# A linear attention block with an FFN on one core: another opening, the first two FFNs in tile 3, and another order in the last three tiles

## The reference, cut to what matters

```python
def attention(x, W_attn, b_attn, W_proj, b_proj):        # x: 8 x 1024 x 512
    q, k, v = split(x @ W_attn + b_attn, 3)               # 16 heads of 32
    q, k = elu(q) + 1, elu(k) + 1
    # over the tokens t of a sequence:
    #   kv += k_t (outer) v_t ; ksum += k_t
    #   y_t = (q_t . kv) / (q_t . ksum + 1e-6)
    return y @ W_proj + b_proj

def ffn(x, weight, bias):
    x16 = clip(x, -448, 448).astype(float8_e4m3fn).astype(float16)
    w16 = clip(weight, -448, 448).astype(float8_e4m3fn).astype(float16)
    return (x16 @ w16.T).astype(float32) + bias

x = x + attention(layernorm(x), ...)
x = x + ffn(layernorm(x), ...)
```

## Time and profile before

| what | value |
|---|---|
| median of 3 executions | 950.37 us (949.42 to 951.35) |
| the profiled execution's own time | 948.85 us |
| its span, first to last instruction | 947.1 us |
| TensorE busy | 918.2 us, 97% |
| DVE, ACT, POOL busy | 731.8, 745.6, 641.3 us (77, 79, 68%) |
| DMA moved | 99.12 MB, mean 105 GB/s |

### The profile page before, as it was taken

The page is one execution under the profiler, slowest core; times in us unless marked ns, Lnnn a source line. Parts: engine busy times, 40 slices in busy tenths (PEclk is TensorE's granted clock), DMA queues, the critical chain, the costliest instruction groups (busy, mean ns, idle before and its releaser), DMA issues.

```text
span 947.1 us, 44776 instructions
## 1 busy us (share of the span) xinstructions
PE 918.2 (97%) x19470; PEld 490.5 (52%) x19532; DVE 731.8 (77%) x1404; ACT 745.6 (79%) x1358; POOL 641.3 (68%) x713
## 2 busy tenths in 40 slices
PE   5998999999999999999999999999999999999896
PEld 2455555555555555555555555555555555555454
DVE  6999879787777777778687687777778687676687
ACT  5788787877869688787877868788787878868874
POOL 5659877766767677676776667677676676764433
PEclk9999999999999999999999999999999999999999
DMA  8926564565464554565555465555555455462421
GB/s 268 143 41 109 109 119 103 97 119 97 95 122 100 98 116 104 96 114 105 95 114 107 91 116 106 89 118 108 92 114 112 89 114 110 90 103 59 76 69 59
DMA packets 252036, 99.12 MB, mean 105 GB/s; under 512 B 232384, under 2 KB 232640, under 8 KB 251840
## 3 DMA queue, kind: packets, MB, share of 16 engines
q1 hardware_dynamic: 251840, 96.25, 52.3%
HBM read 22.81 MB, written 16.78 MB: 42 GB/s over the span
## 4 chain that ended last, share of the span: by engine, by line
PE 90%; POOL 3%; issue 2%; ACT 2%; DVE 2%; SPq 1%; DMA 1%; ACTq 0%; POOLq 0%
PE R L235 77%; PE S L235 13%; POOL st L1029 1%; POOL xn L1031 1%; DMA x2t<-x2b 0%; ACT raw L477 0%; POOL xs L1076 0%; PE R L239 0%; DVE raw L739 0%; POOL raw L1062 0%; DMA xs<-in_L_attn_x 0%; ACT ktok L477 0%; SPq L1227 0%; DVE v L728 0%; ACT o L477 0%
## 5 line engine op out<-in xcount | busy, mean ns | idle before, releaser
L235 PE MATMUL R<-xt,wh 128*128 128x512 f16 x1024 | 306.2, 381 | 2.4 <-ACT wh L477 2.4
L716 DVE SCALAR_TENSOR_TENSOR qk<-qk,rel 128x512 f32<-128x512 f32 x128 | 112.8, 884 | 118.1 <-ACT rel L489 118.1
L477 ACT ACTIVATE raw<-qk 64x512 f32<-64x512 f32 x256 | 160.8, 628 | 48.9 <-PE S L235 45.7
L235 PE MATMUL R<-xt,wl 128*128 128x512 f16 x512 | 194.0, 380 | 0.0
L1083 POOL TENSOR_TENSOR yhl<-y,yhl 128x512 f16<-128x512 f32 x60 | 70.0, 1167 | 146.1 <-ACT yhl L477 146.1
L235 PE MATMUL R<-wh,xt 128*128 128x512 f16 x512 | 158.0, 379 | 0.0
L235 PEld LDWEIGHTS R<-xt,wh 128*128 128x128 f16 x1024 | 96.7, 98 | 116.0 <-DVE xt L882 2.6
L739 DVE TENSOR_TENSOR raw<-S,causal 64x1024 f32<-64x1024 f32 x128 | 155.9, 1218 | 0.9
L1029 POOL TENSOR_TENSOR st<-st,half 128x1 f32<-128x1 f32 x127 | 92.7, 730 | 90.6 <-DVE st L705 89.8
L235 PE MATMUL R<-wph,yt 128*128 128x512 f16 (+1 forms) x520 | 132.4, 377 | 3.9 <-ACT yt L477 1.9
L486 ACT ACTIVATE qk<-R,bqk,wm 128x512 f32<-128x512 f32 x128 | 98.9, 773 | 35.6 <-PE R L235 35.0
(11 more groups left out here) (108 smaller groups left out, 1364.8 us busy)
## 6 DMA issues: line engine op xcount, KB each, us to landing
xs<-in_L_attn_x SPq DMA_DIRECT2D x64, 256.0 KB, 3.1
out<-xs SPq DMA_DIRECT2D x63, 256.0 KB, 2.4
raw<-in_L_attn_W_attn SPq DMA_DIRECT2D x3, 1024.0 KB, 9.5
xs<-in_L_attn_W_proj SPq DMA_DIRECT2D x4, 256.0 KB
raw<-in_L_ffn_weight SPq DMA_DIRECT2D x1, 1024.0 KB, 17.0
raw<-raw SPq DMA_TRANSPOSE x63, 3.7
x2t<-x2b SPq DMA_TRANSPOSE x62, 2.5
xt<-xnhl SPq DMA_TRANSPOSE x60, 3.5
```

The costliest lines, as they stand in the source:

```text
L235: return e.matmul(out, a, b, start=start, stop=stop, skip_group_check=True)
L477: return e.activation(out, in_, ACT.Copy, **more)
L716: e.scalar_tensor_tensor(qk[j % 2][:, i, :], qk[j % 2][:, i, :], 1.0, rel[:, (u - 1) % 2, :], ALU.min, ALU.add).then_inc(s_phi, 1)
```

## The change

- **Opening.** The attention weight comes in four pieces (256, 256, 512 and 512 columns) with a size and a scale each instead of three, and its high and low parts are made in eight parts (four of 128 columns, four of 256). TensorE does warming transposes of the identity (16, 3 and 4) around the first four tiles' transposes, and `most(1)` inside the first product. ACT and DVE have a new order.
- **Tiles 0 to 3.** On ACT in tile 0 one feature product goes ahead of the projection's high part, and the third feature product and `values(0)` ahead of `queries(1)`. On DVE `proj_weight` goes from tile 0 to tile 1, `ffn_high` to tile 1, `ffn_round` to tile 2; the four sums go to POOL in tile 2. `t_wf` goes to SyncE's tile 3, behind `t_k(5)`; `ffn(0)` is done in tile 3 with `ffn(1)` on TensorE, ACT and DVE. The stores of tiles 0 to 2 are issued in tile 4 and the load of tile 14 in tile 5.
- **POOL's add_bp** is done once a tile in tiles 1 to 7 and twice in tiles 8 to 15, instead of twice in 0 to 7.
- **Last three tiles.** DVE does yt's low part and y ahead of v's result, and the FFN's residual sum one tile later; `ln2(61)` goes to tile 63. POOL does `spread(63)` ahead of `proj(61)`, and stores follow one tile later.

```diff
+PIECES = ((0, 256), (256, 512), (512, 1024), (1024, 1536))
+
+PARTS = ((0, 128), (128, 256), (256, 384), (384, 512), (512, 768), (768, 1024), (1024, 1280), (1280, 1536))
...
@@ TensorE
-                        pe.wait_ge(s_wl, i // 2 + 1)
+                        pe.wait_ge(s_wl, part_of(i) + 1)
...
                     if i == j == 0 and m == 8:
+                        most(1)
                         pe.wait_ge(s_wl, 1)
...
-            for m in range(4):
-                t1(m)
+            warm(16)
+            t1(0)
+            t1(1)
+            warm(3)
+            t1(2)
             most(0)
+            t1(3)
+            warm(4)
             for i in range(12):
                 proj_qkv(0, i)
-                if i in (0, 2, 11):
-                    most((0, 2, 11).index(i) + 1)
+                if i in (1, 4, 11):
+                    most((1, 4, 11).index(i) + 2)
...
-                elif 2 <= n < NT - 1:
+                elif n == 3:
+
+                    ffn(0)
+                    ffn(1)
+                elif 4 <= n < NT - 1:
                     ffn(n - 2)
@@ ACT
             t1(0)
             t1(1)
+            attn_size(0)
             t1(2)
-            attn_size(0)
             t1(3)
             attn_weight(0)
             attn_weight(1)
             attn_size(1)
-            phi(0, 0)
+            attn_size(2)
             attn_weight(2)
             attn_weight(3)
+            phi(0, 0)
+            attn_weight(4)
             phi(0, 1)
+            attn_weight(5)
...
-                    ahead(chunks(n)[0])
+                    if n == 0:
+                        ahead(chunks(n)[0][:1])
+                        proj_weight()
+                        ahead(chunks(n)[0][1:])
+                        k_tokens(n + 1)
+                        ahead(chunks(n)[1])
+                        values(n)
+                        queries(n + 1)
+                        ln1_parts(n + 8)
+                    else:
+                        ahead(chunks(n)[0])
@@ DVE, opening
             t1_parts(0)
             t1_parts(1)
+            scale(0)
             t1_parts(2)
-            scale(0)
             t1_parts(3)
             attn_weight(0)
             attn_weight(1)
-            v_peak()
             scale(1)
+            attn_weight(2)
+            attn_weight(3)
+            scale(2)
+            phi(0, 0)
             ln1(4)
-            attn_weight(2)
-            phi(0, 0)
-            attn_weight(3)
+            attn_weight(4)
             ln1(5)
             phi(0, 1)
-            scale(2)
+            v_peak()
+            attn_weight(5)
             phi(0, 2)
+            scale(3)
+            phi(0, 3)
             ln1(6)
-            attn_weight(4)
-            phi(0, 3)
+            attn_weight(6)
+            phi(0, 4)
+            attn_weight(7)
             ln1(7)
-            attn_weight(5)
-            phi(0, 4)
-            v_scale()
             phi(0, 5)
             phi(0, 6)
+            v_scale()
             phi(0, 7)
@@ DVE, main loop
                 if n < NT:
+                    if n == 1:
+                        ahead(chunks(0)[1])
                     if not tail(n):
                         scores(n)
+                    if n == 1:
+                        proj_weight()
                     if n + 8 < NT:
                         ln1(n + 8)
-                    if n == 0:
-                        proj_weight()
                     if n == 1:
-                        ffn_sum(0, 2)
+                        ffn_high()
+                    if n == 2:
+                        ffn_round()
+                    if tail(n - 1):
+
+                        t_y(n - 1)
+                        if n == NT - 1:
+                            ln2(n - 2)
+                        values(n)
                     ahead(chunks(n)[0])
-                    if tail(n - 1):
-                        t_y(n - 1)
                     if n:
                         ahead(chunks(n)[1])
-                    values(n)
-                    if n == 0:
-                        ffn_high()
-                        ffn_round()
-                        ahead(chunks(n)[1])
+                    if tail(n - 1):
+                        if n < NT - 1:
+                            ffn(n - 3)
+                    else:
+                        values(n)
                 if 1 <= n < NT:
                     proj(n - 1)
                 if n == NT - 1:
+                    ffn(n - 3)
                     t_y(n)
-                if 1 <= n < NT:
+                if 1 <= n < NT and n != NT - 2:
                     ln2(n - 1)
@@ POOL
+            def ffn_sum(f):
+                pool.wait_ge(s_wfd, 3)
+                e.tensor_tensor(w_b[:, f, :], w_hi[:, f, :], w_lo[:, f, :], ALU.add).then_inc(s_wfs, 1)
...
+                    if n == 2:
+                        ffn_sum(0)
+                        ffn_sum(1)
                     if n:
                         values(n)
...
                 if 1 <= n < NT:
                     add_bf(n - 1)
+                if n == 2:
+                    ffn_sum(2)
+                    ffn_sum(3)
@@ SyncE
             def t_wf(f):
-                sp.wait_ge(s_wfd, 4 + f)
+                sp.wait_ge(s_wfs, f + 1)
...
-                if n == 1:
-                    t_wf(0)
-                    t_wf(1)
                 if n + 2 < NT:
                     t_k(n + 2)
...
                 if n == 1:
                     t_y(n)
-                    t_wf(2)
-                    t_wf(3)
-                if n + 10 < NT:
+                if n == 3:
+                    for f in range(4):
+                        t_wf(f)
+                if n == 5:
+                    load_x(n + 9)
+                if n != 4 and n + 10 < NT:
                     load_x(n + 10)
```

More of the change, by code:

```diff
@@ L141, in build @@
         Y = S[:, :, 4 * HALF:4 * HALF + 4 * W]
-        UN = [wm[:, 7 * i + 4:7 * i + 5] for i in range(4)]
-        UP = [wm[:, 7 * i + 5:7 * i + 6] for i in range(4)]
-        UN_V, UN_P = wm[:, 33:34], wm[:, 34:35]
+        UN = [wm[:, 7 * i + 4:7 * i + 5] for i in range(5)]
+        UP = [wm[:, 7 * i + 5:7 * i + 6] for i in range(5)]
+        UN_V, UN_P = wm[:, 41:42], wm[:, 42:43]
         raw_p = xs[:, NX - 4:NX, :]
@@ L162, in build @@
         s_out = [sem(f"xo{i}") for i in range(NX)]
-        s_wa = [sem(f"wa{i}") for i in range(3)]
+        s_wa = [sem(f"wa{i}") for i in range(4)]
         s_wf, s_wp, s_bqk, s_bva, s_bias = sem("wf"), sem("wp"), sem("bqk"), sem("bva"), sem("bias")
@@ L187, in build, with weights @@
         s_rs1, s_xn, s_rs2, s_x2, s_xb, s_x1b = sem("rs1"), sem("xn"), sem("rs2"), sem("x2"), sem("xb"), sem("x1b")
-        s_yl, s_blank, s_one, s_khl, s_near = sem("yl"), sem("blank"), sem("one"), sem("khl"), sem("near")
+        s_wfs, s_yl, s_blank, s_one, s_khl, s_near = sem("wfs"), sem("yl"), sem("blank"), sem("one"), sem("khl"), sem("near")
         bank = {}
+        def weights(first, end):
+            third, at = divmod(first, D)
+            return raw[:, third, :, at:at + end - first]
         def four(t):
@@ L500, in proj_size @@
                 act.wait_ge(s_wp, 64)
-                e.activation(wpl[:, :, :].bitcast(BF16), raw_p, ACT.Abs, accum_out=wm[:, 21:22]).then_inc(s_size, 1)
+                e.activation(wpl[:, :, :].bitcast(BF16), raw_p, ACT.Abs, accum_out=wm[:, 28:29]).then_inc(s_size, 1)
             def attn_weight(i):
-                cols = slice(i * 256, (i + 1) * 256)
-                of = slice(i % 2 * 256, i % 2 * 256 + 256)
-                act.wait_ge(s_up, i // 2 + 1)
-                copy(wh[:, :, cols], raw[:, i // 2, :, of], scale=UP[i // 2]).then_inc(s_wh, 1)
+                piece = piece_of(PARTS[i][0])
+                act.wait_ge(s_up, piece + 1)
+                copy(wh[:, :, slice(*PARTS[i])], weights(*PARTS[i]), scale=UP[piece]).then_inc(s_wh, 1)
             def proj_weight():
-                act.wait_ge(s_up, 4)
-                copy(wph[:, :, :], raw_p, scale=UP[3]).then_inc(s_wph, 1)
+                act.wait_ge(s_up, 5)
+                copy(wph[:, :, :], raw_p, scale=UP[4]).then_inc(s_wph, 1)
             def ffn_half():
-                act.wait_ge(s_wl, 4)
+                act.wait_ge(s_wl, part_of(7) + 1)
                 act.wait_ge(s_wfc, 4)
@@ L687, in _ @@
                     spread(n + 1)
-                if 2 <= n <= NT and not (n < NT - 1 and tail(n)):
+                if n == 3:
+                    ffn(0)
+                    ffn(1)
+                elif 4 <= n <= NT and not (n < NT - 1 and tail(n)):
                     ffn(n - 2)
@@ L933, in ffn_round @@
                                 saturate=False).then_inc(s_wfd, 1)
-            def ffn_sum(first, end):
-                dve.wait_ge(s_wfd, 3)
-                for f in range(first, end):
-                    e.tensor_tensor(w_b[:, f, :], w_hi[:, f, :], w_lo[:, f, :], ALU.add).then_inc(s_wfd, 1)
             e.memset(pair[:, :], 0.0).then_inc(s_pair, 1)
@@ L1020, in _ @@
```

(28 more changed lines are left out.)

98 lines of the change are left out of this document (46 added, 52 removed).

## The result

The changed kernel takes 958.05 us (median of 4 runs, 957.0 to 959.05) where the kernel before took 950.86 us in runs of the same chip (4 runs, 949.42 to 951.57). The ratio is 1.0073, 95% interval 1.0057 to 1.009: **slower by 7 us**, where I forecast 3.6. The profiled execution has a span of 956.2 us and its own time is 957.9.

The account below looks back on a forecast made before the run. The prediction took TensorE to bound the kernel, so only its idle or slow time counts. Front +3.1, clock +2.0 and last tiles -1.5 gave +3.6 us on the median of 950.37: 954.0 us, range 947.5 to 958.5.

Parts of the forecast that it names:

- the step that decides: Tile 3: TensorE, at ffn(0) at 99.5, waits 8.0 us for the FFN weight's transposes, there at 107.5.
- Opening: Up to the k transposes: DVE's list ends at 42.4 instead of 44.60, a gain of 2.3 us, bounds 0.8 and 4.
- whether the clock came up or not: Opening: the 2.3 us gain was claimed to hold with TensorE's clock fast or slow.
- Tile 2's two waits: TensorE's waits at tile 2's masked scores (1.22 us) and first FFN (1.25 us) were both to go.
- proj_weight (L916, 2.34 us) goes to tile 1: Tiles 0 to 2: this move adds 2.34 us to DVE's stretch in tile 1, with y at 73.3.
- The clock: Behind tile 3's long wait: TensorE's matmuls run slow, costing 2.0 us, bounds 0 and 2.07.
- The tail: Last tiles: yt's low part first on DVE removes a TensorE wait, -1.5 us, bounds -0.5 and -2.3.
- the 1.18 us gap stays nearly whole: Last tiles: TensorE's wait at 929.04 for ACT's yt stays almost unchanged, as ACT's queue ends just ahead of it.
- In time: Rival: t_k(5) is through before 94, the FFN weight lands before TensorE's 99.5, total 944.1 us; chance 0.16.
- The clock stays up: Rival: tile 3's long wait is there but TensorE's clock doesn't fall, total 952.0 us; chance 0.16.
- the opening gives nothing: Rival: DVE stays where it was in the opening, smaller pieces come later, total 955.5 to 957 us; chance 0.12.

Follow-up runs that it names:

- e10: The changed kernel once more, with no edit, on another chip: 957.63 us, ratio 1.0081.
- e7: e5 with DVE's v_scale behind the last feature product instead of ahead of it: 950.64 us, ratio 1.0012.
- e9: e5 without the 23 warming transposes: 952.05 us, ratio 1.0021.
- e1: The changed kernel with the four FFN weight transposes ahead of t1(11) and t_k(5) in SyncE's tile 3: 948.51 us, ratio 0.998.
- e5: e1 with POOL's spread(1) moved ahead of k_split(2) and the low part of tile 8 in tile 0: 947.22 us, ratio 0.9974.
- e2: The changed kernel with 64 warming transposes on TensorE ahead of ffn(0) in tile 3: 956.82 us, ratio 1.0073.
- e4: The kernel before with only the new order of the last tiles: 948.14 us, ratio 0.9986.
- e11: e5 with the last tiles as before the change: 948.14 us, ratio 0.9977.
- e6: e5 with 12 more warming transposes on TensorE ahead of the k transposes in tile 0: 950.67 us, ratio 1.0009.
- e8: The kernel before with only the warming transposes (16, 3 and 4) and the summing matmul behind the fourth tile's transposes: 951.09 us, ratio 1.0012.

## Why the prediction was right, and where its sizes were off

The direction was right, and so was the step that decides; the size was half: +3.6 us forecast, +7.2 and +6.9 measured by the medians. That 958.05 lies in the range at all is in part luck: my upper end of 958.5 was there for a rival that didn't happen, and the forecast by itself went to 957. I go by e10's profile, whose span is 7.3 us above that of before, 6.7 of it in front of update(4) and 0.6 behind it.

- **Opening, right in size: -2.2** (k transposes 42.51 in e10, 42.97 in the first; forecast 42.4). DVE's list is the last to end, as argued, from its first scale at 11.2 (10.7 forecast) to 42.4, with 2.8 us idle (2.4 forecast), but by less than a microsecond: e7 takes 3.8 us out of its way and wins 0.17, or about 0.8 with the executions' difference taken off. And "whether the clock came up or not" was wrong. e9 puts the price of the clock at 3.1 us at this point. I had taken DVE's list as a chain that TensorE doesn't touch; in fact each feature product waits for TensorE's projection through ACT, so slow projections delay the same list. It was the wait between the engines that I had wrong. Without the fast level the new opening would have been 1 us worse than the old.
- **Tile 2's two waits, right:** 1.22 and 1.25 us are gone, in every kernel with the new order.
- **"proj_weight (L916, 2.34 us) goes to tile 1": the step that failed.** I priced this move, and ffn_high's, as time of DVE alone. Beside them POOL's low part and spread(1) take 2.67 and 2.77 us instead of 1.15 and 0.62, and TensorE's values(1) waits 1.46 us for the latter (e10, e1); e5 takes the wait away by reordering POOL alone. What I said of ACT's moved values and queries held: ACT's high part of y ends at 61.3 in e10 and at 63.6 in the kernel before. But POOL was missing among its readers.
- **The step that decides, right: 7.8 to 8.4 us of wait against 8.0.** e1 takes it away by SyncE's order alone and gains 9 us. But both ends came later than written: TensorE was at ffn(0) at 101.77 instead of 99.5, by the 1.46 us and another pause of 0.58, which ends 1.4 us after a fetch like those at the end; the weight was there at 109.6 instead of 107.5. Several terms of the latter were off. Norm 10 began at 81.4, not 79.3: DVE's statistics for it ended at 80.8, and POOL had work up to 81.4. The four POOL sums took 1.07 us each, not 1.25 (2.15 and 2.14 for two), so that the split of keys ended at 101.1 instead of 100.0. The first of the four transposes went out at 102.65, where my sum has 101.2, and TensorE went on half a microsecond after the last had landed (issued at 106.6, 2.5 us to landing). As both ends moved together, the wait kept its length and **update(4) moved by the whole 2 us**.
- **The clock, right: 1.5 us against 2.0.** Seven matmuls take 3.17 to 3.19 us after the long wait and 1.67 without one (e1, e2), and clock 0.51 against 1.00 in the windows over them. The Trainium skill (TensorE: Matmul & The Clock Gate, What's actually happening) says that an idle array falls back to half rate. The trace agrees in this place: a granted clock of 0.51 after 7.83 idle us, and 1.00 where the same time was filled with transposes.
- **The tail, right by itself (e4: 1.3 to 1.9 us faster; forecast 1.5), wrong in this kernel.** From update(58) to the end of the span e10 is 0.8 us longer than before. By its rows: the pause of 1.86 us of values(59) is gone; the wait for yt's low part, 1.2 us, is gone; from update(62) to update(63) it takes 3.1 us more, 2.42 of it the pause at the two score matmuls and 0.7 the slow FFN matmuls behind it (1.49 us for three, elsewhere 0.81); and the end loses 0.8, mainly as ACT's yt is 2.28 us late instead of 1.18. My reasoning "the 1.18 us gap stays nearly whole" fell too: it doubled. ACT's queue is why: its two yt copies start 8.2 us apart with no gap between them, with the old tail and the new (e11), so TensorE, which no longer waits for DVE, waits for ACT instead. No run made ACT's queue shorter.
- **The rivals.** "In time" fell: the first t_wf left at 102.65, not before 94, though e1 shows what it would have been worth, and its 948.5 is well above my 944.1: the 1.46 us, the 1.28 us left at ffn(0) and a tail that gained nothing weren't in that sum. "The clock stays up" is refuted by the windows, "the opening gives nothing" by 2.2 us.

In sum for e10, in front: -2.2 (opening) + 1.46 (spread) - 1.22 - 1.25 + 7.83 + 0.58 + 1.5 (clock) = +6.7, the 6.7 of update(4); behind it +0.6. Against the forecast of +5.1 and -1.5 the front misses by 1.6 us (2.1 of arrival, less 0.5 of clock) and **the tail by 2.1, the larger part**: the term that was mis-sized most is the -1.5 of the last tiles, which came out at +0.6.

What stays open: why some fetches come too late and most don't (the pause at the end is 1.3 to 2.4 us long at the same place, and the fetch in it starts 0.3 to 0.9 us ahead of it and takes 0.9 to 1.5); and how much of e6's loss is the padding itself.

## What to carry to other kernels

When a transfer is moved to a later tile, write down what stands ahead of it in its in-order queue and when the last of that can be issued, then do the same for every queue that reads what an engine now does later: here three moved lines on SyncE were worth 9 us, and one moved call on POOL about 1 more by the rows. Where a short wait grows long on TensorE, add the matmuls behind it at the lower clock (1.5 us here). Where a DVE operation moves, look also at what POOL does beside it. Where two chains end close together, a gain on one is worth only the distance to the other. And judge an edit near the end of a program by runs with and without it on both bodies, since a handful of instructions more at the start can move a pause of 2 us in or out of the part that is looked at.

## What the runs showed of the hardware that I had not expected

- **Pauses of TensorE of 1.2 to 2.4 us that no engine and no transfer of the kernel releases, placed by the count of instructions.** Twelve more transposes at the start moved one by exactly twelve matmuls, 870 us later (e6). Each ends 1.2 to 1.6 us after the end of a 16 KB instruction fetch, and their places lie 126 to 127 weight loads or a multiple of that apart.
- **They can cost the clock too, but not always.** After the pause of 2.42 us in e10 three FFN matmuls took 1.49 us, after that of 2.16 us in the first profile 0.81. After the pause in values(59), 1.86 us in the kernel before and 1.87 in e4, four matmuls took 1.04 and 1.89. After the 1.51 us at 62.77 of the first profile the projections ran slow; the windows over the same work in tile 1 and tile 2:

```profile
63.14:72.70 9.56, 9.56 (x39) 3.88 (x36) 9.32 (x9) 7.74 (x16) 8.60 (x6) 0.82 0.62 112
78.16:86.03 7.87, 7.87 (x42) 3.43 (x36) 7.57 (x15) 6.92 (x14) 6.88 (x8) 1.00 0.91 152
```

  That is 1.7 us lost at a granted clock of 0.82, on top of the pause.
- **The same 23 warming transposes can help or not.** In the new opening the first product took 1.89 us in seven kernels, after gaps of 0.49 to 1.07 us, and 2.13 and 2.15 in e1 and e7 after 0.49. In e8, where gaps of 1.28 and 1.52 us stand ahead of it, it took 3.53.
- **A POOL operation can stretch fourfold beside DVE.** spread, 64 x 264 elements, takes 0.62 us in e5 and 2.77 in e1 beside DVE's ffn_high; a low part takes 1.16 elsewhere and 2.67 to 2.78 beside proj_weight. Each ends about its own time after DVE's operation does (0.5 us for spread, 1.0 for the low part in e1 and e5), as if POOL had stood still until DVE was done. In e5 it is add_bp that stands beside ffn_high, and it takes 3.44 us, against a mean of 1.32.
